# Graph network on one core: order of the own products, bf16 planes and register reads in the three mean layers

## The chip, the core and the metric

The program runs on one core of a Trainium2 chip. The metric is the device time of one execution in microseconds (us). The kernel before has a median of 7610.16 us over three runs (7602.88 to 7610.16).

## What is computed

Four graph modules follow each other over 6250 nodes with 128 features and 106250 edges (both directions of 50000 edges, and a loop at each node), sorted by destination. After each module there is a residual and a layer norm. The change concerns the third module alone, three "mean" layers:

```python
def sage_conv(h, Wl, b, Wr):
    agg = jax.ops.segment_sum(h[src], dst, num_segments=n) * inv_deg
    return agg @ Wl + b + h @ Wr
h = jax.nn.relu(sage_conv(x, W_l0, b0, W_r0))
h = jax.nn.relu(sage_conv(h, W_l1, b1, W_r1))
return sage_conv(h, W_l2, b2, W_r2)
```

The other modules (a gated recurrent layer, three attention layers, a tensor-product message layer) have the same text before and after.

## The kernel before, in words

Nodes lie in 49 blocks of 128, in 13 groups of four blocks (the last has one). Below, layers 0, 1 and 2 are the three mean layers. Each sums the rows of source nodes into a buffer of destination columns (`agg`, the first part of `sums`), in two ways.

- **Dense.** An adjacency matrix in bf16, made earlier, lies in DRAM. TensorE multiplies it with the node rows, which are split into three bf16 planes (line 1925), so that the float32 value is kept. There are 115 steps (`pe_dense`). The first 17 hold three blocks each and give 544 "extra" columns, one for each of 544 tiles of edges; the other 98 are two halves of 49 blocks with 5 banks of 418 columns. The queue of SyncE reads the adjacency through four slots.
- **Sums of a quad.** 288 tiles of 128 edges are gathered by GpSimd (line 1939, one indirect DMA each), four to a quad, 72 quads. ScalarE makes one-hot matrices (lines 1947, 1950), TensorE multiplies (line 1961, three banks in turn), and VectorE adds each of the four results to a window of `agg` whose start column is read from memory into a register (`window_at`, line 741, one load for four starts; the add is line 2026). Gathers use 16 slots: quad q+4 is gathered once quad q is multiplied. TensorE may be three quads ahead of VectorE's adds.
- **Extra adds.** The 544 extra columns are copied from the banks after step 17 (`keep_extras`, line 2009), and VectorE adds them one column at a time at register addresses (line 1992), 8 after each quad's adds, four starts to a register load. Each add to `agg` waits for the one before it, since windows can overlap. The halves of the dense part are added by `add_half` (line 2001), and line 2035 closes the layer.

Ahead of the sums comes a layer's head. In layers 1 and 2 TensorE makes the product of the last sums (line 1825), VectorE mixes it with the "own" term (line 1834), ScalarE applies Relu (line 2155) and issues the store of the rows. TensorE turns the rows (line 1856), ScalarE keeps them (line 1861) in `xT`; TensorE then makes the own product of a group (line 1871), and VectorE stores it with its bias (line 1880) in `hT`, over the node rows, for which reason a group's planes must be made first. Of a group's planes ScalarE makes the first, a bf16 copy (lines 2160, 2090), and VectorE the other two and a rest (lines 1845, 1846, 1848). TensorE puts up to 13 dense steps between the turns and own products. VectorE sets `agg` to zero (line 2147, in layer 0 line 2077). In layer 0 the head is the layer norm of the module before.

The order is that of the code. Each engine has its own queue and waits on semaphores. `quads_by(n)` says how many quads TensorE has multiplied after n dense steps: before the change none until step 13, and then 72 spread over 102 steps.

## Time and profile before

| what | us |
|---|---|
| median of the runs | 7610.16 |
| the profiled execution, whole | 7606.87 |
| its span | 7605.1 |
| layer 0 of the mean layers, 5054 to 5507.4 (with the norm) | 453.4 |
| layer 1, 5507.4 to 5940.7 | 433.3 |
| layer 2, 5940.7 to 6387.8 | 447.1 |

The page gives the busy time of each engine over the whole span. Which engine sets the pace of a stage is not read from it, but from the timelines: an engine can be idle half of the time between instructions that wait for each other. A timeline row merges equal instructions: its start, the time from the first start to the last end, their number, and in brackets the idle time ahead and what ended it. Register loads belong to the sequencer and don't count as busy.

### The profile page before, as it was taken

What the parts mean: (1) busy time and instruction counts of PE and PEld (TensorE: products, weight loads), DVE (VectorE), ACT (ScalarE), POOL (GpSimd) and SP (SyncE); (2) the same over time, 40 slices, a digit from 0 to 9 for tenths busy, and PEclk for the clock granted to TensorE, in tenths of its full rate; (3) what the DMA queues carried; (4) which work ended last, traced back from release to release, by engine and by line L of the source; (5) the groups of instructions that cost most, each with busy time, mean ns of one, the idle gap of its engine ahead of it and who ended that gap; (6) DMA issues with size and microseconds to landing.
All of it is one profiled execution on the core that took longest, in us unless ns stands there. A gap on an engine that the chain in (4) does not pass through costs nothing. (4 is left out here: it accounts for less than half of the span.)

```text
span 7605.1 us, 137273 instructions
## 1 busy us (share of the span) xinstructions
PE 5586.2 (73%) x30113; PEld 4217.7 (55%) x30114; DVE 4809.0 (63%) x20423; ACT 2121.2 (28%) x5508; POOL 5100.1 (67%) x5173
## 2 busy tenths in 40 slices
PE   5664454667767777776777766769899897898887
PEld 4432223345656655666655556656566654676665
DVE  7974433555666655666754766674454545888887
ACT  1033332131111141111141111143343332555554
POOL 5788772447777747777747777737657474777774
PEclk6687777877888787888887888889999998989988
DMA  9422232146677746777746767756667574222222
GB/s 308 122 68 63 71 76 53 36 126 197 205 207 205 205 148 194 208 206 205 209 152 188 210 206 206 206 151 207 176 198 211 161 216 120 55 55 55 55 54 52
DMA packets 911521, 1149.47 MB, mean 151 GB/s; under 512 B 143137, under 2 KB 676193, under 8 KB 911009
## 3 DMA queue, kind: packets, MB, share of 16 engines
q1 hardware_dynamic: 689200, 673.54, 29.4%
q0 software_dynamic: 202464, 461.07, 22.6%
q10 hardware_dynamic: 19346, 9.66, 0.5%
q14 instruction: 388, 3.18, 0.1%
q8 instruction: 123, 2.02, 0.1%
HBM read 882.09 MB, written 261.74 MB: 150 GB/s over the span
## 5 line engine op out<-in xcount | busy, mean ns | idle before, releaser
L486 POOL DMA_INDIRECT G<-table_kv,idx x2496 | 2377.4, 952 | 959.1 <-issue 762.3
L1554 DVE SCALAR_TENSOR_TENSOR sums<-ramp,place,bank 128x128 f32<-128x128 f32 x2496 | 721.9, 343 | 1001.1 <-PE bank L1501 813.5
L1939 POOL DMA_INDIRECT G<-table_h,src_idx x864 | 824.6, 954 | 485.4 <-issue 256.3
L1473 ACT COPY slab<-bank 128x512 f32<-128x512 f32 x624 | 364.9, 585 | 2485.0 <-PE bank L1492 2480.4
L1492 PE MATMUL bank<-ident,G 128*128 128x128 f32 x2496 | 627.7, 338 | 570.9 <-DMA G<-table_kv,idx 565.2
L1501 PE MATMUL bank<-qT,slab 128*128 x4992 | 916.2, 341 | 166.1 <-issue 144.4
L486 POOL DMA_INDIRECT G<-table_h,idx x832 | 835.4, 1004 | 299.3 <-issue 231.3
L534 PE MATMUL bank<-OH,sums 128*128 128x128 f32 x4992 | 858.7, 327 | 143.4 <-DVE sums L523 122.1
L1501 PEld LDWEIGHTS bank<-qT,slab 128*128 128x128 f32 x4992 | 810.6, 246 | 258.4 <-issue 257.9
L514 DVE TENSOR_SCALAR OH<-ramp,place,weight 128x128 f32<-128x128 f32 x2262 | 805.2, 359 | 151.2 <-issue 81.2
L534 PEld LDWEIGHTS bank<-OH,sums 128*128 128x128 f32 x4992 | 763.7, 234 | 195.0 <-issue 73.0
L1492 PEld LDWEIGHTS bank<-ident,G 128*128 128x128 f32 x2496 | 388.6, 167 | 762.5 <-DMA G<-table_kv,idx 725.0
L868 POOL DMA_INDIRECT adjacency<-sums x544 | 657.2, 1208 | 165.8 <-issue 165.8
L523 DVE TENSOR_TENSOR sums<-sums,bank 128x128 f32 x2496 | 697.4, 279 | 48.7 <-DVE sums L523 18.1
L1925 PE MATMUL bank<-sums,qT 128*128 128x418 bf16 (+1 forms) x3528 | 673.7, 333 | 31.6 <-DVEq L2004 10.9
L2401 PEld LDWEIGHTS bank<-OH,qT 128*128 128x128 f32 x3328 | 471.5, 225 | 283.0 <-DVE sums L2479 252.7
L2401 PE MATMUL bank<-OH,qT 128*128 128x128 f32 x3328 | 506.1, 315 | 123.9 <-DVE sums L2479 122.3
L849 POOL DMA_INDIRECT G<-table_gated,src_idx x288 | 284.1, 987 | 307.3 <-PE bank L973 176.2
L1925 PEld LDWEIGHTS bank<-sums,qT 128*128 128x128 bf16 x3528 | 346.7, 98 | 255.6 <-issue 35.7
L1992 DVE TENSOR_TENSOR sums<-sums,rows 128x1 f32 x1632 | 265.7, 163 | 347.8 <-DVE sums L2026 108.6
L1947 ACT ACTIVATE OH<-ramp,place 128x128 f32<-128x128 f32 x864 | 275.8, 390 | 676.1 <-PE bank L1961 674.1
L997 PE MATMUL bank<-slab,hT 128*128 128x418 f32 (+1 forms) x592 | 244.3, 566 | 294.9 <-DVE slab L1088 294.8
(342 smaller groups left out, 8868.2 us busy)
## 6 DMA issues: line engine op xcount, KB each, us to landing
stash<-G SPq DMA_DIRECT2D x312, 512.0 KB
sums<-stash SPq DMA_DIRECT2D x624, 256.0 KB
sums<-adjacency SPq DMA_DIRECT2D x294, 522.5 KB
adjacency<-same SPq DMA_DIRECT2D x49, 1184.0 KB
same<-adjacency SPq DMA_DIRECT2D x90, 522.5 KB
G<-table_kv,idx POOLq DMA_INDIRECT x2496
sums<-adjacency SPq DMA_DIRECT2D x48, 408.0 KB
table_kv<-G SPq DMA_DIRECT2D x72, 256.0 KB, 3.1
```

The lines of the kernel that those rows point to most:

```text
L486: pool.indirect_dma_start(G[:, s, 0:width], None, tab, bass.IndirectOffsetOnAxis(ap=idx[:, s:s + 1], axis=0)).then_inc(c_gather[s].sem, 16)
L514: ins = dve.tensor_scalar(OH[:, s, :], ramp[:], place[:, tile], w, ALU.is_equal, ALU.mult)
L523: dve.tensor_tensor(w, w, bank[banks[q_add % len(banks)]][:, k * P:(k + 1) * P], ALU.add).then_inc(c_added.sem, 1)
L534: ins = pe.matmul(bank[banks[q % len(banks)]][:, (s % QUAD) * P:(s % QUAD + 1) * P], view[:, s, :], OH[:, s, :], start=True, stop=True)
L868: pool.indirect_dma_start(adj_cells, bass.IndirectOffsetOnAxis(ap=cell[:, d:d + 1], axis=0), count[:, d:d + 1], None).then_inc(scattered[i ...
L1473: act.copy(quad(KT, q).rearrange("p s d -> p (s d)"), bank[q % 2][:, :]).then_inc(c_kt.sem, 1)
L1492: ins = pe.transpose(bank[q % 2][:, (s % QUAD) * P:(s % QUAD + 1) * P], G[:, s, 0:D], ident[:])
L1501: ins = pe.matmul(bank[2 + q % 2][:, (s % QUAD) * P:(s % QUAD + 1) * P], KT[:, s, :], w, start=True, stop=True)
L1554: ins = dve.scalar_tensor_tensor(scratch[:, s % QUAD, :], ramp[:], place[:, bass.ds(t * SLOTS + s, 1)], bank[2 + q % 2][:, (s % QUAD) * P: ...
L1925: ins = pe.matmul(bank[c][:, 0:width], plane[k][:, b * P:(b + 1) * P], adj_slot[s][:, j * at + c * width:j * at + (c + 1) * width], start= ...
L1939: pool.indirect_dma_start(G[:, s, 0:D], None, table[l], bass.IndirectOffsetOnAxis(ap=src_idx[:, DENSE + t:DENSE + t + 1], axis=0)).then_in ...
L2401: ins = pe.matmul(o, msg[:, s, part * D:(part + 1) * D], OH[:, s, :], start=True, stop=True)
```

## The change

The own term goes to `xT`, where the turned rows stood, so that it no longer overwrites the node rows. Own products come ahead of nearly all planes. VectorE makes the first plane, no longer ScalarE. GpSimd sets `agg` to zero behind its 16th gather. TensorE does no dense step before all own products are done; `pe_all_sums` then runs 115 steps with 2 quads ahead and 70 spread over all of them. The extra columns come 12, 8, 8 after a quad, from quad 12 on (before: 8, from quad 4 on). All register loads of a quad, two or three for its extra columns and one for its windows, are read ahead of the wait for TensorE. In layer 2 the residual is loaded into `nodes_h`.

```diff
+        own_h = xT[:].rearrange("p (b d) -> p b d", d=D)
...
-                                               nodes_h[:, b0 + j, :], ALU.mult, ALU.add)
+                                               own_h[:, b0 + j, :], ALU.mult, ALU.add)
...
-            dve.tensor_tensor(hT[:, four(g)].rearrange("p (b d) -> p b d", d=D),
+            dve.tensor_tensor(xT[:, four(g)].rearrange("p (b d) -> p b d", d=D),
...
+        def dve_first_planes(ready):
+            for g in range(GROUPS):
+                b0, nb = blocks_of(g)
+                ready(g, b0 + nb - 1)
+                dve.tensor_copy(plane[0][:, four(g)], hT[:, four(g)]).then_inc(first_plane.sem, 1)
 
         def dve_own_and_planes(l):
+            dve_planes(0)
+            done = 1
             for g in range(GROUPS):
                 dve_own(g, l)
-                if g + PLANES_AHEAD < GROUPS:
-                    dve_planes(g + PLANES_AHEAD)
+                if g % 3 == 2:
+                    dve_planes(done)
+                    done += 1
+            for g in range(done, GROUPS):
+                dve_planes(g)
...
-            return 2 + (n - GROUPS) * (RUN_QUADS - 2) // (STEPS - GROUPS) if n > GROUPS else 0
+            return 2 + n * (RUN_QUADS - 2) // STEPS
...
+                if t == SLOTS - 1:
+                    sums_used()
+                    pool.memset(agg, 0.0).then_inc(agg_zero.sem, 1)
...
+        def pe_all_sums():
+            for q in range(quads_by(0)):
+                pe_sum_quad(q)
+            for n in range(STEPS):
+                pe_dense(n)
+                for q in range(quads_by(n), quads_by(n + 1)):
+                    pe_sum_quad(q)
...
-        EXTRAS_A_QUAD = 8
+        def extras_by(q):
+            n = max(0, q - EARLY_QUADS)
+            return min(DENSE, 8 * n + 4 * -(-n // 3))
...
                 windows = window_at(DVE, DENSE + q * QUAD, QUAD)
+                columns = [c for d in range(extras_by(q), extras_by(q + 1), QUAD) for c in window_at(DVE, d, QUAD)]
+                if q == 0:
+                    dve.wait_ge(agg_zero.sem, agg_zero.at(1))
                 dve.wait_ge(c_rows.sem, c_rows.at(q + 1))
...
-                if q >= EARLY_QUADS and extras_left[0]:
-                    add_extras(min(EXTRAS_A_QUAD, extras_left[0]))
+                if columns:
+                    add_extras(extras_by(q), columns)
...
-                        sp.wait_ge(own_rows.sem, own_rows.at(GROUPS))
-                        sp.dma_start(xT[:].rearrange("p (b d) -> p b d", d=D), table[0].rearrange("(b p) d -> p b d", p=P)).then_inc(residual_in.sem, 16)
+                        sp.wait_ge(planes_ready.sem, planes_ready.at(GROUPS))
+                        sp.wait_ge(rows_stored.sem, rows_stored.at(16 * ROW_STORES))
+                        sp.dma_start(nodes_h, table[0].rearrange("(b p) d -> p b d", p=P)).then_inc(residual_in.sem, 16)
```

On TensorE, in layer 1 before, an own product of a group (line 1871) and a dense step (line 1925, three blocks) take turns:

```order
L1871 MATMUL bank<-wts,xT 128x128 [waits own_kept,turned_kept]
L1871 MATMUL bank<-wts,xT 128x128 x3
L1925 MATMUL bank<-sums,qT 128x272 [waits planes_ready,adjacency_in2]
L1925 MATMUL bank<-sums,qT 128x272 x3
L1925 MATMUL bank<-sums,same 128x272 x2
```

At the same place after the change the last own product (now line 1874) is followed by the sums of quads 0 and 1 (line 1976), and the first dense step (line 1937) stands behind these:

```order
L1874 MATMUL bank<-wts,xT 128x128 [waits own_kept,turned_kept]
L1976 MATMUL bank<-OH,G 128x128 [waits gather0,own_kept,onehot_ready]
L1976 MATMUL bank<-OH,G 128x128 [waits gather1]
L1976 MATMUL bank<-OH,G 128x128 [waits gather2]
L1976 MATMUL bank<-OH,G 128x128 [waits gather3]
L1976 MATMUL bank<-OH,G 128x128 [waits gather4,own_kept,onehot_ready]
L1976 MATMUL bank<-OH,G 128x128 [waits gather5]
L1976 MATMUL bank<-OH,G 128x128 [waits gather6]
L1976 MATMUL bank<-OH,G 128x128 [waits gather7]
L1937 MATMUL bank<-sums,qT 128x272 [waits planes_ready,adjacency_in0]
```

So 13 dense steps moved from among the turns and own products to behind them, and quads start at once.

On VectorE, before, each register load of a quad stands where its addresses are used (rows that repeat are left out; ISA is the register arithmetic of an address):

```order
L741 TENSOR_LOAD start
L2026 ISA [waits added,extra_added,rows_used]
L2026 TENSOR_TENSOR sums<-sums,bank 128x128
...
L741 TENSOR_LOAD start [waits added]
L1992 ISA [waits extra_added]
L1992 TENSOR_TENSOR sums<-sums,rows 128x1
```

After the change three or four loads stand in a row ahead of a quad's first wait:

```order
L742 TENSOR_LOAD start x4
L2051 ISA [waits added,extra_added,rows_used]
L2051 TENSOR_TENSOR sums<-sums,bank 128x128
...
L2014 ISA [waits extra_added,added]
L2014 TENSOR_TENSOR sums<-sums,rows 128x1
```

The number of loads is the same, 72 for windows and 136 for extra columns a layer; the latter moved from among the adds and extra adds to the front of the quad.

## Rows read from the trace of the kernel before

**Rows 1.** The page: busy time, share of the span and instructions of each engine.

```profile
PE 5586.2 (73%) x30113; PEld 4217.7 (55%) x30114; DVE 4809.0 (63%) x20423; ACT 2121.2 (28%) x5508; POOL 5100.1 (67%) x5173
```

**Rows 2.** Busy by stretch: stretch, length, PE, PEld, DVE, ACT, POOL, PEclk, DMA, GB/s.

```profile
5528.50:5532.60 4.10, 4.05 (x19) 2.81 (x20) 4.03 (x7) 0.87 (x2) 2.99 (x4) 0.50 0.19 51
5590.50:5745.50 155.00, 153.22 (x949) 98.46 (x948) 75.86 (x373) 61.16 (x161) 117.21 (x125) 1.00 0.72 213
```

**Rows 3.** VectorE timeline, a quad late in layer 1: start, length, group, [idle before].

```profile
5886.39 1.54 DVE L2026 TENSOR_TENSOR sums<-sums,bank 128x128 f32 x4 [0.45 <-DVE sums L1992]
5888.46 1.03 DVE L1992 TENSOR_TENSOR sums<-sums,rows 128x1 f32 x4 [0.52 <-DVE sums L2026]
5889.85 1.03 DVE L1992 TENSOR_TENSOR sums<-sums,rows 128x1 f32 x4 [0.35 <-DVE sums L1992]
5891.33 0.71 DVE L2026 TENSOR_TENSOR sums<-sums,bank 128x128 f32 x2 [0.45 <-DVE sums L1992]
```

**Rows 4.** Register loads on VectorE, 5600 to 5900: durations, first and last start.

```profile
L741 DVEq TENSOR_LOAD <-start x177: 339/343/375, 5599.9 to 5899.6; - x177
```

**Rows 5.** VectorE, layer 1: adds of quads 0, 1 and 4, the end.

```profile
5577.40 1.54 DVE L2026 TENSOR_TENSOR sums<-sums,bank 128x128 f32 x4 [2.43 <-PE bank L1961]
5579.25 1.55 DVE L2026 TENSOR_TENSOR sums<-sums,bank 128x128 f32 x4 [0.30 <-DVE sums L2026]
5590.53 1.12 DVE L2026 TENSOR_TENSOR sums<-sums,bank 128x128 f32 x3 [4.00 <-PE bank L1961]
5936.43 3.48 DVE L2001 TENSOR_TENSOR sums<-sums,bank 128x418 f32 x5 [0.41 <-DVE sums L1992]
5940.06 0.59 DVE L2035 TENSOR_TENSOR sums<-sums 128x418 f32<-128x418 f32 x1
```

**Rows 6.** TensorE: first sums of layers 0 and 1, dense steps of both kinds.

```profile
5142.87 1.83 PE L1961 MATMUL bank<-OH,G 128*128 128x128 f32 x15
5576.21 1.95 PE L1961 MATMUL bank<-OH,G 128*128 128x128 f32 x16
5577.99 0.63 PE L1925 MATMUL bank<-sums,qT 128*128 128x272 bf16 x4
5580.11 1.05 PE L1961 MATMUL bank<-OH,G 128*128 128x128 f32 x8
5895.62 1.95 PE L1925 MATMUL bank<-sums,qT 128*128 128x418 bf16 x10
5898.29 0.88 PE L1925 MATMUL bank<-sums,qT 128*128 128x418 bf16 x4
```

**Rows 7.** ScalarE: end of the norm, last Relu, a cast, a kept group.

```profile
5090.51 2.16 ACT L2090 CAST qT<-hT 128x512 bf16<-128x512 f32 x4
5525.01 0.31 ACT L2155 ACTIVATE hT<-hT 128x128 f32<-128x128 f32 x1 [0.44 <-ACT hT L2155]
5526.74 0.62 ACT L2160 CAST qT<-hT 128x512 bf16<-128x512 f32 x1
5527.26 0.59 ACT L1861 COPY xT<-bank 128x512 f32<-128x512 f32 x1
```

**Rows 8.** VectorE, head of layer 1: one plane operation of two groups.

```profile
5526.39 0.69 DVE L1845 TENSOR_TENSOR sums<-hT,qT 128x512 f32<-128x512 f32 x1 [2.77 <-ACT qT L2160]
5528.33 0.68 DVE L1845 TENSOR_TENSOR sums<-hT,qT 128x512 f32<-128x512 f32 x1
```

**Rows 9.** Groups by line: a single-source operation on VectorE, a memset on GpSimd.

```profile
L1218 DVE TENSOR_SCALAR start<-start 128x832 int32<-128x832 int32 x1 | 0.6, 587 | 0.0
L2265 POOL MEMSET wts<- 128x768 f32 x1 | 0.7, 737 | 41.8 <-PE bank L1825 41.8
```

**Rows 10.** GpSimd, gathers of layer 1: durations, first and last start.

```profile
L1939 POOL DMA_INDIRECT G<-table_h,src_idx x272: 939/944/953, 5577.5 to 5915.9; - x136
```

**Rows 11.** Layer 2: both engines at the adjacency read behind the residual.

```profile
6107.53 3.67 PE L1925 MATMUL bank<-sums,qT 128*128 128x418 bf16 x10 [4.46 <-DMA sums<-adjacency]
6116.88 1.13 DVE L2026 TENSOR_TENSOR sums<-sums,bank 128x128 f32 x3 [8.29 <-PE bank L1961]
```

More of the change, by code:

```diff
@@ L250, in build_program @@
         first_plane = signal("first_plane_ready")
+        agg_zero = signal("sums_zero")
         planes_ready = signal("planes_ready")
@@ L1979, in after_extra, with add_extras @@
                     dve.wait_ge(c_extra.sem, c_extra.at(n[1]))
-            extras_left = [DENSE]
-            def add_extras(k):
+            def add_extras(first, columns):
                 after_adds()
-                done = DENSE - extras_left[0]
-                extras_left[0] -= k
-                for d in range(done, done + k, QUAD):
-                    windows = window_at(DVE, d, QUAD)
-                    for j in range(QUAD):
-                        after_extra()
-                        w = agg[:, bass.ds(windows[j], 1)]
-                        dve.tensor_tensor(w, w, extra[:, d + j:d + j + 1], ALU.add).then_inc(c_extra.sem, 1)
-                        n[1] += 1
+                for d, column in enumerate(columns, first):
+                    after_extra()
+                    w = agg[:, bass.ds(column, 1)]
+                    dve.tensor_tensor(w, w, extra[:, d:d + 1], ALU.add).then_inc(c_extra.sem, 1)
+                    n[1] += 1
             def add_half(half):
@@ L2027, in dve_sums @@
                     n[0] += 1
-                if q >= EARLY_QUADS and extras_left[0]:
-                    add_extras(min(EXTRAS_A_QUAD, extras_left[0]))
+                if columns:
+                    add_extras(extras_by(q), columns)
                 if l == 2 and q == half_quads + 4:
                     dve.wait_ge(residual_in.sem, residual_in.at(16))
-                    dve.tensor_tensor(hT[:], hT[:], xT[:], ALU.add)
+                    dve.tensor_tensor(xT[:], xT[:], hT[:], ALU.add)
             add_half(1)
@@ L2076, in _, with normalized @@
                 dve.sem_inc(order_ready.sem, 1)
-                dve.memset(agg, 0.0)
-                for g in range(PLANES_AHEAD):
-                    dve_planes(g)
+                def normalized(g, b):
+                    dve.wait_ge(norm_dve.sem, norm_dve.at(b // 2 + 1))
+                    dve.wait_ge(norm_act.sem, norm_act.at((b + 1) // 2))
+                dve_first_planes(normalized)
                 dve_own_and_planes(0)
@@ L2086, in _ @@
                 for g in range(GROUPS):
-                    b0, nb = blocks_of(g)
-                    act.wait_ge(norm_dve.sem, norm_dve.at((b0 + nb - 1) // 2 + 1))
-                    act.wait_ge(norm_act.sem, norm_act.at((b0 + nb) // 2))
-                    act.copy(plane[0][:, four(g)], hT[:, four(g)]).then_inc(first_plane.sem, 1)
-                    if g >= 3:
-                        act_keep_turned(g - 3)
-                for g in range(GROUPS - 3, GROUPS):
                     act_keep_turned(g)
@@ L2106, in _ @@
                     pe_turn(g, normalized)
-                n = 0
                 for g in range(GROUPS):
                     pe_own(g, 0)
-                    if n < GROUPS:
-                        pe_dense(n)
-                        n += 1
-                for n in range(n, STEPS):
-                    pe_dense(n)
-                    for q in range(quads_by(n), quads_by(n + 1)):
-                        pe_sum_quad(q)
+                pe_all_sums()
         norm_passed()
@@ L2138, in _ @@
                 def _(_e):
-                    pool_rows(l)
+                    pool_rows(l, lambda: pool.wait_ge(filled.sem, filled.at(GROUPS)))
                 @block.vector
@@ L2144, in _ @@
                         dve_mix(g, PRODUCT_BANKS[g % 3])
-                    for g in range(PLANES_AHEAD):
-                        dve_planes(g)
-                    dve.memset(agg, 0.0)
+                    dve_first_planes(lambda g, b: dve.wait_ge(rows_ready.sem, rows_ready.at(g + 1)))
                     dve_own_and_planes(l)
@@ L2159, in _ @@
                     for g in range(GROUPS):
-                        act.copy(plane[0][:, four(g)], hT[:, four(g)]).then_inc(first_plane.sem, 1)
                         act_keep_turned(g)
@@ L2165, in _ @@
                 def _(_e):
-                    n = 0
                     for g in range(GROUPS):
@@ L2170, in _ @@
                         pe_turn(g, lambda g, b: pe.wait_ge(rows_ready.sem, rows_ready.at(g + 1)))
-                        while (n + 1) * FIRST_BLOCKS <= g // 2 * QUAD and n + 1 < GROUPS // 2:
-                            pe_dense(n)
-                            n += 1
                     for g in range(GROUPS):
                         pe_own(g, l)
-                        if n < GROUPS:
-                            pe_dense(n)
-                            n += 1
-                    for n in range(n, STEPS):
-                        pe_dense(n)
-                        for q in range(quads_by(n), quads_by(n + 1)):
-                            pe_sum_quad(q)
+                    pe_all_sums()
             sums_passed()
```

10 lines of the change are left out of this document (4 added, 6 removed).

## The prediction

> **What bounds the kernel now.** I read the page first, then the busy times by stretch, then the timelines of the mean layers, which is where the reader should look, too. By the page TensorE is the busiest engine, 73% [rows 1], and in the first part of layer 1's sums it is busy 153.2 of 155 us, VectorE only 75.9 [rows 2]. That reading misleads. In the timeline of VectorE each add waits for the one before it, and nothing else [rows 3]: four adds, a register load, four extra adds, a load, four extra adds, a load, and the next quad's adds begin 4.94 us after those before (5886.39 to 5891.33), with no wait for TensorE in brackets. Two other engines are close: TensorE needs 1.5 half steps of 2.67 us and one quad of 0.89, 4.9 us [rows 6]; a gather starts every 1.25 us (5577.5 to 5915.9, 271 steps), 5.0 us a quad [rows 10]. So three engines run in step, and VectorE, with the extra adds to do, holds the layer's end: from the first add of quad 4 at 5590.5 to the last operation's end at 5940.65 are 350.1 us [rows 5].
>
> The parts of VectorE's 4.94 us are needed below [rows 3]. Starts of adds are (1.54 - 0.29) / 3 = 0.42 apart (the last add alone is 0.29), of extra adds (1.03 - 0.16) / 3 = 0.29. From the first add to the first extra add are 2.07: a load after the adds costs 2.07 - 4 x 0.42 = 0.39. That is the load's own 0.343 [rows 4] and 0.05 around it. From one group of extra adds to the next are 1.39, so the load between them costs 1.39 - 4 x 0.29 = 0.23, since it partly lies beside an extra add that runs.
>
> **The change, part by part.**
>
> *Register reads.* What TensorE has ready costs VectorE no wait, so reading ahead of the wait hides nothing while VectorE is the late one [rows 3]. It even costs: the load that stood between extra adds for 0.23 now stands behind another load. No row shows two loads in a row. Below, it could be 0.05, the gap alone, if loads overlapped; above, 0.39, a load in series [rows 3, 4]. I take 0.39, the row nearest: after the adds the load also delays what stands behind it by its whole length. 133 such loads a layer (136 less the three of quad 12, which fall into a wait) at 0.39 are 51.9 us; before, 68 x 0.39 + 68 x 0.23 = 42.1. Plus 9.8. A quad with 8 extra columns now takes 5.1 us, one with 12 takes 6.3 (four more extra adds at 0.29), and the one ahead of it 5.5 for its fourth load: 16.9 for three.
>
> *The head.* In layer 1 the last Relu ends at 5525.3 [rows 7]. Before, ScalarE made a cast and a kept group in turn, 0.50 each; now 13 kept groups alone, 6.5 us, and an own product of 0.9 on TensorE: the first own result can be stored at about 5533. VectorE meanwhile makes 13 first planes from 5523.7 on. A copy of 512 float32 to bf16 is not in the trace. Below, it takes 512/832 of 0.587, 0.36 [rows 9]; above, 0.65, as a plane operation does. Even at 0.65 it is done, with one group of planes, by 5534: no cost in layer 1, and 0 to 3 us in layer 0, where the norm ends at 5090.5 [rows 7]; I take 1.5. From 5532.7 (5525.3 + 6.5 + 0.9) come 12.25 own results at 0.61 to 0.65 (8 us) and four groups of planes at 1.94 [rows 8] (7.8), and about 1.5 for the handovers: the last own result is stored at 5550.0, and quad 0 starts there, against 5576.2 before [rows 6]. That is 26.2 earlier. Layer 2 has the same head. Layer 0: 5090.5 + 6.5 + 0.9 + 1.5 + 17.3 = 5116.7, against 5142.9, also 26.2 earlier.
>
> *What is no longer done in the head.* Before, 13 dense steps ran among the own products, and the extra columns were ready 14.3 us after quad 0 (quad 4's first add at 5590.5, 5576.2 for quad 0). Now TensorE has all of it behind quad 0: 17 steps of 2.12 (5577.99 to 5580.11), 36.0; quads 0 to 12, 13 x 0.89 = 11.6; two half steps, 5.3 [rows 6]. Two waits come in. Quad 3 needs quad 0 added, and VectorE first has eight groups of planes to make (14.4, a load and adds 1.9), while TensorE is at quad 3 after 11.1: 5.2 us. And the extra columns are copied behind the adds of quad 11: 2.6. Together 60.7 from quad 0 to the first add of quad 12, 46.4 more than the 14.3 before.
>
> *What is left from there.* Eight quads are already added, at 1.85 each [rows 5]: 14.8 us less; the loads add 9.8. So 350.1 becomes 345.1, 5.0 less.
>
> *The zeroing.* GpSimd's memset of 768 elements took 0.74 [rows 9], which gives 6 us for 6668 in proportion. It stands behind the 16th gather (about 5548) and ends ahead of VectorE's first add (about 5566). Twice that would still end in time in layer 1, and cost 0 to 2 us in layer 0. VectorE's own memset lay in an idle stretch of the head; taking it off brings nothing but is contained in the head's sum. The Trainium skill ("GPSIMD Engine Reference", "Key points") says that GpSimd shares its SBUF interfaces with VectorE and contends with it where VectorE has two SBUF inputs, as the planes have; by it the upper figure is the likelier. No row here has the two side by side.
>
> *The residual.* In layer 2 the big read ahead of step 41 makes TensorE late, and VectorE waits 8.3 us [rows 11] (its cycle is 7.9 longer than 4.94). TensorE now needs 1.64 x 2.67 + 0.89 = 5.28 a quad where VectorE needs 5.64, and after 14 quads is 5.0 us ahead. That much of the wait goes.
>
> *Sum.* Layers 0 and 1: -26.2 + 46.4 - 5.0 = +15.2 each. Layer 2: 15.2 - 5.0 = +10.2. In all +40.6 on the profiled execution's 7606.9, 7647.5. The median of the runs shown is 3.3 above that execution, 7610.2, so the forecast is **7651**.
>
> **The rivals.**
>
> *A, the forecast:* VectorE stays the late engine, and starts its long stretch of extra adds 20 us later than before with only 5 us less to do.
>
> *B, loads cost little, TensorE sets the pace; faster.* If the sequencer takes the next load up while one is under way, a load in a row costs 0.05. VectorE's three quads then take 16.9 - 10 x 0.34 = 13.5 us, TensorE's 15.8, and TensorE has everything behind an earlier quad 0: 36.0 + 98 x 2.67 + 72 x 0.89 + waits of 10 are 371.8 us, then 6 for the last adds and the half (5936.43 to 5940.65 is most of it [rows 5]). Layer 1 ends at 5550.0 + 377.8 = 5927.8, 12.9 earlier, layer 0 12.8, layer 2 (which keeps its wait for the adjacency) 18.7 earlier, 44.4 in all: 7566. The total turns at 40.6 / 399 loads = 0.10 below my price, at 0.29 a load; below 0.28 TensorE is the bound. For it speaks that reading ahead of a wait is free where the wait is real, and that TensorE is busy 99% of a stretch already. Against it: behind a load the next instruction came a whole load later wherever the timeline lets me see it [rows 3], and the wait would have to be real, which it isn't.
>
> *C, the clock stays low in the head; slower still.* Before, dense steps kept TensorE busy through the head, and its granted clock was 1.00 afterwards, but 0.50 (the 1.2 GHz level) in the 4 us after its idle time [rows 2]. Now turns and own products alone fill three quarters of its time or less. At the lower level an own product of a group takes 1.8 us against the 1.2 that VectorE needs on average, 13 x 0.55 = 7 us later a layer, 21 in all: 7672. The Trainium skill ("TensorE: Matmul & The Clock Gate", "Part 1: The HAM clock gate") says that the clock follows how busy the engine has lately been; by it this case is possible, and the row of before agrees that idle time brings the lower level.
>
> *D, nothing measurable.* The head gains more than I see (a copy at 0.36, quad 3 not late because its planes end sooner), 10 to 13 us a layer: 7610 to 7620.
>
> **How the numbers follow.** Chances: A 0.60, B 0.15, C 0.15, D 0.10. Between A and C all is slower; B is faster; D is mostly within 0.2%, 15 us, which is about what a measurement of this kernel can tell from no change. Slower 0.75, same 0.08, faster 0.17. The unknown costs (0 to 9 for copies, 0 to 2 for the memset, -7 to +7 for my waits of a few us a layer) put A between 7627 and 7667. The range goes up past C to 7684 and down to 7590, which leaves out B.
>
> **What would show it.** Right: two or three quarters of the way through a layer VectorE shows a cycle of 5.1, 5.5 and 6.3 us a quad, no wait for TensorE in it, and TensorE idle between quads; loads in a row 0.39 apart; quad 0 in layer 1 about 43 us after the layer's start, where it was 69; quad 12's first add about 103 after it; layers of 469, 448 and 457 us. Wrong: VectorE's adds wait for TensorE's sums through the long stretch (B, and then the layer has 420 us), or loads in a row start 0.05 apart; TensorE at 0.50 while it turns rows and makes own products (C); quad 12 at less than 92 us (D). GpSimd should no longer be busy back to back.

## The result, and the profile after

The changed kernel takes 7642.87 us (median of 6 runs, 7633.51 to 7659.43), the kernel before in the same comparison 7606.68 (6 runs, 7594.99 to 7610.16). The ratio is 1.0052, with a 95% interval of 1.0039 to 1.0065: slower by half a per cent. Its profiled execution took 7643.14 us, with a span of 7641.3; the span before was 7605.1, so 36.2 us are to be explained.

I read the views in the same order as before. First the page's busy line, which answers to [rows 1]:

```profile
PE 5561.5 (73%) x30113; PEld 4192.3 (55%) x30114; DVE 4799.4 (63%) x20459; ACT 2105.1 (28%) x5469; POOL 5124.5 (67%) x5176
```

No engine's busy time has grown by more than 25 us: ScalarE has 16 less (its casts went), GpSimd 24 more (17.0 of it three memsets). The 36 us are waiting time and no work. The same holds of the stretch of [rows 2] in layer 1 (stretch, length, busy time of PE, PEld, DVE, ACT, POOL, then PEclk, DMA, GB/s):

```profile
5590.50:5745.50 155.00, 152.47 (x998) 102.43 (x996) 64.59 (x310) 57.22 (x150) 115.66 (x123) 0.99 0.74 217
```

TensorE looks as full as before, VectorE still emptier, and yet VectorE holds the end. Its timeline shows it. These are quads in that stretch (start, length, group, idle before), which answer to [rows 3]:

```profile
5702.17 1.55 DVE L2051 TENSOR_TENSOR sums<-sums,bank 128x128 f32 x4 [1.20 <-PE bank L1976]
...
5707.29 1.55 DVE L2051 TENSOR_TENSOR sums<-sums,bank 128x128 f32 x4 [1.20 <-issue]
5708.97 2.19 DVE L2014 TENSOR_TENSOR sums<-sums,rows 128x1 f32 x8
5712.73 1.54 DVE L2051 TENSOR_TENSOR sums<-sums,bank 128x128 f32 x4 [1.56 <-issue]
...
5715.63 2.49 DVE L2014 TENSOR_TENSOR sums<-sums,rows 128x1 f32 x9 [0.48 <-DVE sums L2014]
5719.31 1.55 DVE L2051 TENSOR_TENSOR sums<-sums,bank 128x128 f32 x4 [1.20 <-issue]
...
5724.38 1.55 DVE L2051 TENSOR_TENSOR sums<-sums,bank 128x128 f32 x4 [1.19 <-issue]
```

A quad with 8 extra columns takes 5.12 (5702.17 to 5707.29) and, at best, 5.07 us (5719.31 to 5724.38), the one with a fourth load behind it 5.44 (5707.29 to 5712.73). The one with 12 columns took 6.58 here, with a gap of 0.48 among its extra adds, and 6.24 where it has no such gap (5627.83 to 5634.07, in the next view of VectorE). The gap of 1.20 ahead of the adds is three register loads in a row, and 1.56 is four. "issue" means that no semaphore was late; where the brackets name TensorE the gap is no longer, so this wait is none either. The loads themselves, in the gap behind 5706.1 (durations, first and last start):

```profile
L742 DVEq TENSOR_LOAD <-start x3: 342/343/345, 5706.0 to 5706.7; - x3
```

Three loads start within 0.7 us. The fourth lengthens the gap from 1.20 to 1.56 and the quad from 5.07 to 5.44: a load in a row costs 0.37, its whole length and 0.03 more.

Now the head of layer 1, which starts where layer 0's last operation ends, at 5524.5, 17.2 later than in the kernel before. VectorE, answering to [rows 5] and [rows 8]: first planes, first own result, last plane, first add, the adds of quads 12 and 13, the end.

```profile
5539.85 4.24 DVE L1890 CAST qT<-hT 128x512 bf16<-128x512 f32 x13
...
5551.07 1.51 DVE L1882 TENSOR_TENSOR xT<-bank,bias_rows 128x512 f32<-128x512 f32 x2 [5.06 <-PE bank L1874]
...
5580.70 0.32 DVE L1851 TENSOR_TENSOR same<-sums,qT 128x128 bf16<-128x128 f32 x1
5581.28 1.54 DVE L2051 TENSOR_TENSOR sums<-sums,bank 128x128 f32 x4 [0.25 <-issue]
...
5627.83 1.55 DVE L2051 TENSOR_TENSOR sums<-sums,bank 128x128 f32 x4 [8.34 <-PE bank L1976]
...
5634.07 1.55 DVE L2051 TENSOR_TENSOR sums<-sums,bank 128x128 f32 x4 [1.20 <-issue]
...
5964.58 2.04 DVE L2023 TENSOR_TENSOR sums<-sums,bank 128x418 f32 x3 [0.50 <-DVE sums L2051]
5968.30 0.60 DVE L2060 TENSOR_TENSOR sums<-sums 128x418 f32<-128x418 f32 x1
```

And TensorE there, answering to [rows 6]: quads 0 and 1, the first dense step, quad 3, and the first half step behind the copy of the extra columns.

```profile
5566.86 3.75 PE L1976 MATMUL bank<-OH,G 128*128 128x128 f32 x16 [2.82 <-issue]
5570.41 1.11 PE L1937 MATMUL bank<-sums,qT 128*128 128x272 bf16 x4
...
5582.93 1.13 PE L1976 MATMUL bank<-OH,G 128*128 128x128 f32 x8 [2.27 <-issue]
...
5619.63 3.53 PE L1937 MATMUL bank<-sums,qT 128*128 128x418 bf16 x10 [2.53 <-DVE rows L2031]
```

Quad 0 stands 42.4 us behind the layer's start (5566.9 less 5524.5), where it was 68.9; quad 12's first add follows 61.0 behind quad 0; from there to the end are 341.1. So the layer took 444.4 us against 433.3. The three mean layers take 456.3, 444.4 and 454.1, where they took 448.0, 433.3 and 447.1: +8.3, +11.1 and +7.0, together 26.4 (layer 0 is counted here from its first operation on VectorE, shown below, and not from 5054 as in the table of before). Another 8.9 us lie ahead of them, in code that the change does not touch. The first operation of mean layer 0 on VectorE in the changed kernel, and then in the kernel before:

```profile
5068.23 2.23 DVE L2096 TENSOR_TENSOR qT<-hT,sums 128x448 f32<-128x448 f32 x4 [0.32 <-PEq L1711]
```

```profile
5059.29 2.23 DVE L2071 TENSOR_TENSOR qT<-hT,sums 128x448 f32<-128x448 f32 x4 [0.32 <-PEq L1710]
```

The remaining 1.0 us lies behind the mean layers (36.2 - 8.9 - 26.4).

### The profile page after: what moved, and what is told of

The parts are those of the page before. It is cut to its first block and busy times, and to the rows that moved or that the text cites. A ratio compares the mean times of both kernels' runs of the same rounds, so it can differ in the third digit from the quotient of the medians.

```text
span 7641.3 us, 137448 instructions
## 1 busy us (share of the span) xinstructions
PE 5561.5 (73%) x30113; PEld 4192.3 (55%) x30114; DVE 4799.4 (63%) x20459; ACT 2105.1 (28%) x5469; POOL 5124.5 (67%) x5176
## 5 line engine op out<-in xcount | busy, mean ns | idle before, releaser
L524 DVE TENSOR_TENSOR sums<-sums,bank 128x128 f32 x2496 | 697.8, 280 | 49.8 <-DVE sums L524 18.4
L2051 DVE TENSOR_TENSOR sums<-sums,bank 128x128 f32 x864 | 249.4, 289 | 403.5 <-issue 181.6
```

The lines of the kernel that those rows point to most:

```text
L524: dve.tensor_tensor(w, w, bank[banks[q_add % len(banks)]][:, k * P:(k + 1) * P], ALU.add).then_inc(c_added.sem, 1)
```

## The experiments

They ran on several chips. On one of them the kernel before took 7621.1 us, near its usual time; on others it took 10,127, 9,980 and 9,998. A kernel is only compared with the kernel before that ran beside it, and what the slow chips can and can't tell is said below. "Layer 1" is always from the end of the fold in layer 0 to the end of the fold in layer 1, as above.

### On the chip with the usual time

**Reads back in place.** The changed kernel with each read of four columns just ahead of its four adds:

```diff
-                for d, column in enumerate(columns, first):
-                    after_extra()
+                for g in range(first, last, QUAD):
+                    for d, column in enumerate(window_at(DVE, g, QUAD), g):
+                        after_extra()
```

> The kernel after with the reads of extra columns in their old place, each just ahead of its four adds (the first kernel again, beside the others of this call). Theory A: two or three reads a quad no longer stand in a row, each is 0.14 cheaper between extra adds, and the first no longer delays the next: VectorE's mean quad 5.4 instead of 5.59 us, some 8 to 11 us a layer, 24 to 30 in all: 7613 to 7619, ratio to before 1.001. Rival, reads ahead are free: unchanged, 7643, ratio 1.005.

Measured: 7621.99 us (10 runs), ratio to before 1.0002 (0.9992 to 1.0011). VectorE in this kernel, quads of 8 and of 12 extra columns:

```profile
5703.24 1.55 DVE L2051 TENSOR_TENSOR sums<-sums,bank 128x128 f32 x4 [0.45 <-DVE sums L2015]
5705.31 1.10 DVE L2015 TENSOR_TENSOR sums<-sums,rows 128x1 f32 x4 [0.53 <-DVE sums L2051]
5706.69 1.03 DVE L2015 TENSOR_TENSOR sums<-sums,rows 128x1 f32 x4 [0.28 <-DVE sums L2015]
5708.18 1.55 DVE L2051 TENSOR_TENSOR sums<-sums,bank 128x128 f32 x4 [0.45 <-DVE sums L2015]
...
5714.51 1.55 DVE L2051 TENSOR_TENSOR sums<-sums,bank 128x128 f32 x4 [0.45 <-DVE sums L2015]
```

4.94 us for 8 columns and 6.33 for 12: the mean of three quads is 5.40, where the changed kernel has (5.07 + 5.44 + 6.24) / 3 = 5.58. Times 58 quads that is 10.4 us. From quad 12 to the end layer 1 took 331.2 instead of 341.1, so 9.9 less, and the whole layer 436.4 instead of 444.4. The three layers together are 20.7 us shorter than in the changed kernel (7.1, 8.0 and 5.6), of the 26.4 that these had lost; 5.7 us remain. The changed kernel itself did not run in this comparison, but the one below with the zeroing on VectorE did, and its layer 1 took 341.4 us from quad 12 on, like the changed kernel's 341.1. With the reads back in place the kernel can't be told from the one before: the reading ahead is most of what makes the change slower, and the rest of it, which gains 26 us at quad 0, gives nothing in the end.

**No extra columns.** The changed kernel without the adds and reads of the extra columns:

```diff
-                columns = [c for d in range(extras_by(q), extras_by(q + 1), QUAD) for c in window_at(DVE, d, QUAD)]
...
-                if columns:
-                    add_extras(extras_by(q), columns)
```

> The kernel after, with the extra columns left out: none of the 544 single-column adds of a layer, and none of their 136 register reads. Their products are made on TensorE and copied, but not added, so the sums lack them. It asks who stands next behind VectorE. Theory A (VectorE is the late engine in the changed kernel, TensorE right behind it): VectorE's quad falls from 5.07, 5.45 and 6.24 us to some 2.5, and TensorE takes over with 36.0 + 98 x 2.67 + 72 x 0.89 + about 10 of waits and 6 of tail behind quad 0: a layer of 420 us instead of 444, so about 24 less in each of three, 7571 where the kernel after has 7643 (ratio to the kernel before 0.995). VectorE's adds then wait for TensorE's sums in every quad. Rival, TensorE is the late one already (the mean layers' 26 us come from TensorE's lost head start alone): the time stays within 5 us of the kernel after. Rival, gathers: the gather stream (1.25 us each, 288 of them, from 5564 on) sets the end, then a layer has 410 us and the kernel 7540.

Measured: 7590.23 us (4 runs), ratio 0.9958 (0.9942 to 0.9975); layer 1 took 425.2 us, and 320.8 of them from quad 12 on. VectorE in it, a quad between two half steps:

```profile
5704.75 1.55 DVE L2050 TENSOR_TENSOR sums<-sums,bank 128x128 f32 x4 [4.69 <-PE bank L1976]
5708.31 1.55 DVE L2050 TENSOR_TENSOR sums<-sums,bank 128x128 f32 x4 [2.01 <-PE bank L1976]
```

Here the waits for TensorE are real, 65 of them in the layer's 72 quads: the adds come 3.56 us apart, which is a half step of 2.67 and a quad of 0.89, or 6.23 where two half steps lie between. All of the extra columns' 87.5 us of busy time a layer went, and the layer is only 19.2 us shorter. So VectorE is the late engine of the changed kernel, and TensorE stands right behind it. Where the 19.2 us had lain is seen on TensorE. At the change of halves it waits for VectorE to read its banks, in layer 1 of the changed kernel (first line) and of this one (second):

```profile
PE bank L1937 <- DVEq L2026: 11.2, 1, 11.2
PE bank L1937 <- DVEq L2026: 3.4, 1, 3.4
```

That is 7.8 us less. Ahead of the next layer's first product TensorE stood idle for 16.7 us, now for 7.1, so 9.6 less; and two waits at quads, 1.8 us together, are gone: 19.2 in all. TensorE's account from quad 12's add to the end, without extra columns: 96 half steps of 2.67 and 59 quads of 0.89 are 308.8; 3.4 us it waits at the change of halves for its banks to be read, and 6 us are the tail. That is 318, against 320.8 measured. The gathers were no bound: a layer of 410 us would have been theirs.

**Reads beside adds, early waits away.** The changed kernel with three edits:

```diff
-            return 2 + n * (RUN_QUADS - 2) // STEPS
+            return min(2 + n * (RUN_QUADS - 2) // STEPS, max(3, n - 3))
...
-                if q == EARLY_QUADS:
+                if q == EARLY_QUADS - 1:
                     keep_extras()
...
-                columns = [c for d in range(extras_by(q), extras_by(q + 1), QUAD) for c in window_at(DVE, d, QUAD)]
+                groups, columns = list(range(extras_by(q), extras_by(q + 1), QUAD)), []
...
                     n[0] += 1
+                    if k < len(groups):
+                        columns += window_at(DVE, groups[k], QUAD)
```

> The kernel after with each read of four extra columns issued behind one of the quad's adds (as in the third kernel), and with the two waits of the head taken away: quad 3 is put behind the 7th dense step instead of the 4th, and quads 4 to 8 one behind each step, so that TensorE doesn't stand at quad 3 until VectorE has made its planes; and the extra columns are copied ahead of the adds of quad 11, not behind them. Theory A: the reads beside adds take VectorE's mean quad from 5.59 us to about 5.0, some 30 us of a layer, and the two waits were 5.2 and about 2 us; TensorE is next, at 412 us a layer against 444, so the kernel is at about 7547, ratio to before 0.992. Rival, the head's waits cost nothing because VectorE is late anyway: as the third kernel, 7565 to 7571. Rival, TensorE set the pace already: no gain from the reads, only up to 7 us a layer from the waits: 7622.

Measured: 7579.02 us (4 runs), ratio 0.9943 (0.9922 to 0.9963): faster than the kernel before and, by the ratios, than the changed kernel. VectorE, one quad of 12 columns and the start and end of one of 8:

```profile
5722.34 0.29 DVE L2051 TENSOR_TENSOR sums<-sums,bank 128x128 f32 x1 [1.04 <-PE bank L1976]
...
5724.28 3.44 DVE L2014 TENSOR_TENSOR sums<-sums,rows 128x1 f32 x12
5728.58 0.29 DVE L2051 TENSOR_TENSOR sums<-sums,bank 128x128 f32 x1 [0.85 <-PE bank L1976]
5729.08 0.29 DVE L2051 TENSOR_TENSOR sums<-sums,bank 128x128 f32 x1 [0.22 <-DVE sums L2051]
...
5730.43 2.21 DVE L2014 TENSOR_TENSOR sums<-sums,rows 128x1 f32 x8
5733.10 0.29 DVE L2051 TENSOR_TENSOR sums<-sums,bank 128x128 f32 x1 [0.46 <-DVE sums L2014]
```

With a load beside it an add starts 0.51 us behind the one before, not 0.42: the load costs 0.09 there instead of 0.37. The quad of 8 takes 4.52 us (5728.58 to 5733.10). TensorE in the same kernel has no gap in these rows:

```profile
5724.72 1.94 PE L1937 MATMUL bank<-sums,qT 128*128 128x418 bf16 x10
5726.50 1.05 PE L1937 MATMUL bank<-sums,same 128*128 128x418 bf16 x5
5727.39 1.05 PE L1976 MATMUL bank<-OH,G 128*128 128x128 f32 x8
```

From quad 12 on it took 320.9 us, the same as without any extra columns (320.8): all of their cost now lies beside TensorE. From quad 0 to quad 12's add were 55.1 instead of 61.0, so the two waits gave 5.9, against the 7 expected. I had expected this from waits of 5.2 and 2 us; in the changed kernel's trace they are 2.3 at quad 3 and 2.5 at the copy, and behind the second the half step at the lower clock (3.53 above, 1.94 in this kernel) took some 1.5 longer. The layer took 419.8 us and not the 412 expected, since I had left out three costs that remain: 3.4 us at the change of halves, 1.7 for gathers, and some 2.5 for a low clock at quad 0 (below).

**The zeroing back on VectorE.** The changed kernel with the memset between the first planes and the first group of planes on VectorE, and with neither the memset on GpSimd nor the wait for it:

```diff
                     dve_first_planes(lambda g, b: dve.wait_ge(rows_ready.sem, rows_ready.at(g + 1)))
+                    dve.memset(agg, 0.0)
                     dve_own_and_planes(l)
```

> The kernel after, with the sums zeroed by VectorE again, between the first planes and the first group of planes; nothing on GpSimd, and no wait for it. VectorE's memset of 6668 elements took 5.6 us in the kernel before, GpSimd's 5.7 in the kernel after. Theory (forecast: moving it gives nothing, it fits in idle time of the head): VectorE is through its first planes at about 19.6 us after the layer's start and has its first own result at 25.3; one group of planes, 1.94, and 5.6 of memset end at 27.1, so quad 0 comes 0 to 2 us later, and GpSimd's next gathers 0 to 5 earlier: in all 0 to +6 us against the kernel after. Rival, the memset is on the path, since VectorE has more to do in the head than it had before (13 first planes): +5.6 a layer, +17 in all. Rival, GpSimd's memset holds VectorE up through the shared interfaces: faster than the kernel after by 3 us a layer or more.

Measured: 7657.3 us (4 runs), ratio to before 1.0047 (1.003 to 1.0063), which can't be told from the changed kernel's 1.0052. Its head is more telling than its time. VectorE in layer 1, which starts at 5539.2 there:

```profile
5555.60 4.25 DVE L1890 CAST qT<-hT 128x512 bf16<-128x512 f32 x13
5561.19 5.62 DVE L2157 MEMSET sums<- 128x6668 f32 x1 [1.34 <-issue]
...
5568.59 1.88 DVE L1882 TENSOR_TENSOR xT<-bank,bias_rows 128x512 f32<-128x512 f32 x3
```

The first own result is stored 29.4 us behind the layer's start (5568.59 less 5539.2), where the changed kernel has it at 26.6: most of the memset lies in VectorE's idle 5.06 us, 2 to 3 us don't. Quad 0 came at 44.7 instead of 42.4, and the layers took 5.8, 2.6 and 1.0 us more than in the changed kernel's profile. So the memset on VectorE is not quite hidden in the new head: taking it off gives 2.3 us at quad 0, which my forecast had at nothing of its own. In the total this is less than the comparison can tell. Nothing spoke for the rival in which GpSimd's memset holds VectorE up.

### On the slow chips

Eight runs fell on chips on which every program of this case took about a third longer. There the kernels differed by less, and not in the same way.

**Reads in place, first time.** The same edit as above.

> The changed kernel with the register reads of the extra columns back where they are used (one behind the quad's adds, one between each four extra adds); the reads of the windows stay. Theory (VectorE sets the pace from quad 12 on, and a read in a row costs its whole length, 0.37 us in the changed kernel's trace): 67 reads a layer between extra adds fall from 0.37 to 0.23, 67 behind the adds go from 0.37 to 0.39: 8 us less a layer, some 24 in all, so about 12 us above the kernel before. A cycle of 8 extra columns 4.94, of 12 near 6.5 us. Rival (reads ahead of the wait are hidden, the time goes to TensorE's or GpSimd's new order): no gain over the changed kernel, or slower than it.

Measured: 10,097.9 us, ratio 0.9971 (0.9953 to 0.999), where the usual chip gave 1.0002.

**Before, with reads ahead.** The kernel before with this alone:

```diff
                 windows = window_at(DVE, DENSE + q * QUAD, QUAD)
+                first = max(0, q - EARLY_QUADS) * EXTRAS_A_QUAD
+                groups, columns = list(range(first, min(DENSE, first + EXTRAS_A_QUAD), QUAD)) if q >= EARLY_QUADS else [], []
+                for d in groups:
+                    columns += window_at(DVE, d, QUAD)
                 dve.wait_ge(c_rows.sem, c_rows.at(q + 1))
```

> The kernel before with this part of the change alone: both reads of a quad's extra columns stand behind the read of its windows, ahead of the wait for TensorE. Theory: 68 quads a layer of 5.07 us where 4.94 were, 8 to 9 us a layer more, some 25 in all (7632 where before has 7607). Rival (the reads hide in the wait): the same as before or faster.

> The kernel before with one part of the change alone: the reads of a quad's own and extra columns all stand ahead of its wait for TensorE; head, quads, zeroing and 8 extra columns a quad as before (the second kernel again, on a chip on which the kernel before has its usual time). Theory A: VectorE does not wait there, so three reads in a row cost 0.37 each where those between extra adds had cost 0.23: its quad takes 5.07 us, as the kernel after shows for 8 columns, instead of 4.94. Times 68 quads that is +9 us a layer, +26 in all, ratio 1.0035. Rival, reads ahead of a wait are free or better: ratio 1.000 or less. Rival, VectorE had slack before (the gathers at 5.0 us a quad set the pace, not its 4.94): +0.07 x 68, 5 us a layer, ratio 1.002.

Measured: 0.9997 (0.9977 to 1.0017) and 0.9989 (0.9973 to 1.0006), no difference. But its length of a quad on VectorE can be read wherever a quad does not wait, as here, in the second of the two:

```profile
7806.19 1.54 DVE L2024 TENSOR_TENSOR sums<-sums,bank 128x128 f32 x4 [2.77 <-remote]
7807.86 2.20 DVE L1986 TENSOR_TENSOR sums<-sums,rows 128x1 f32 x8
7811.26 1.54 DVE L2024 TENSOR_TENSOR sums<-sums,bank 128x128 f32 x4 [1.20 <-issue]
```

5.07 us, against 4.94 with the reads in place [rows 3]. The price of the edit is there; on this chip it is mostly covered, since in five of the eight quads around these rows the gap ahead of the adds is 2.1 to 2.9 us and ends with a sum.

**Beside the adds.** The changed kernel and the kernel before, each with the reads behind the quad's first adds (the last of the edits shown for the fastest kernel), and nothing else.

> The changed kernel with each read of four extra columns issued right behind one of the quad's adds of 128 columns, while that add runs. The read of quad 1's windows stood so in the kernel before and cost 0.16 us there. Theory: a cycle of 8 columns costs VectorE 4.65, of 12 columns 6.0, three quads 15.3 us against TensorE's 15.8: TensorE becomes the bound, and a layer ends about 13 us sooner than in the kernel before, 44 in all: 7563 where before has 7607. Rival (the head's new order, GpSimd's memset or the clock is what made the change slow): little gain over the changed kernel, 7620 to 7640.

> The same kernel as in e3 (the changed kernel with each read of four extra columns behind one of the quad's adds), since the first four ran on a chip where the kernel before took 10127 us, with idle time inside TensorE's dense steps that no semaphore ended. Where before takes about 7607, theory: TensorE sets the pace (15.8 us for three quads against VectorE's 15.3), 7563. Rival (not the register reads, but the head, the memset or the clock): 7620 to 7640. If before takes 10127 again, all kernels come within 0.5% of each other and the run settles nothing.

> The kernel after with the reads of extra columns behind the quad's first adds and nothing else (the third kernel again): it takes apart the two edits of the kernel with reads beside adds and without early waits, which had 0.9943 of the kernel before. Theory A: quad 12 stays at 103 us after the layer's start (the waits at quad 3 and at the copy of the extra columns are still there), and from there TensorE sets the pace with 321 us as in that kernel and in the one without extra columns: 424 us a layer, 20 less than the kernel after, ratio 0.9975. Rival, the early waits cost nothing: ratio 0.9943 as there. Rival, only the early waits had brought the gain: 1.0045.

> The kernel before with the same edit: both reads of extra columns stand behind the first two adds of a quad. Theory: VectorE's cycle falls from 4.94 to 4.65, below the 5.0 that four gathers take on GpSimd and the 4.9 of TensorE, so VectorE no longer lags three quads behind and a layer gains its lag, about 11 us, 33 in all (7574). If GpSimd or TensorE had set the pace all along, as the page's busy shares suggest, it gains nothing (7607).

> The kernel before with the reads of extra columns issued behind the quad's first two adds, so that they run beside them; nothing else changed (the fourth kernel again). In the third kernel's profile such a quad of 8 columns took about 4.6 us on VectorE. Theory A with the gathers next: GpSimd's gathers were back to back in the kernel before (16 in 20.0 us without a gap, 5.0 us a quad), and can't go faster, so a layer loses only what lies behind the last gather: about 421 us instead of 433, ratio 0.995; GpSimd busy back to back, VectorE waiting for TensorE's sums. Rival, TensorE next (4.90 a quad): 98 x 2.67 + 68 x 0.89 + 6 = 328 from quad 4 on instead of 350, 411 a layer, ratio 0.991. Rival, VectorE was not the late engine of the kernel before: ratio 1.000. Beside the best kernel so far (0.9943) this says whether the new order of the head is worth anything once the reads are hidden.

Measured: the changed kernel with it has 0.998 (0.9962 to 0.9997), 0.9963 (0.994 to 0.9986) and 0.9961 (0.9947 to 0.9976) in three comparisons; the kernel before with it 0.9993 (0.9969 to 1.0017) and 0.9996 (0.9978 to 1.0013). The first is faster than before in all three, the second in neither. The last two runs had asked what each of the fastest kernel's edits is worth, and whether the kernel before would be as fast with the reads alone; neither is answered for the usual chip. What can be said is local: the quad takes 4.50 us on VectorE in the kernel before, too (in the last of these runs):

```profile
7805.29 0.29 DVE L2022 TENSOR_TENSOR sums<-sums,bank 128x128 f32 x1 [3.30 <-remote]
...
7809.79 0.29 DVE L2022 TENSOR_TENSOR sums<-sums,bank 128x128 f32 x1 [0.42 <-issue]
```

What is different on these chips shows on TensorE. In the first profile with reads ahead in the kernel before, it stood idle in the middle of a half step (first fence), and the view of waits of layer 1 counts 80 such gaps (second: engine, line, what for, us in total, times, longest), where the kernel before has none on that line on its own chip:

```profile
7808.69 0.59 PE L1925 MATMUL bank<-sums,qT 128*128 128x418 bf16 x2
7811.08 0.34 PE L1925 MATMUL bank<-sums,qT 128*128 128x418 bf16 x1 [1.79 <-issue]
```

```profile
PE bank L1925 <- issue: 56.4, 80, 3.4
```

No semaphore ended these gaps, and they are no low clock: over 300 us of sums (7600 to 7900 in the last run of the kernel before beside adds) the granted clock was 0.97. VectorE's, ScalarE's and GpSimd's own durations were the same as on the usual chip (0.29 for an add, 0.95 for a gather). What holds TensorE's instructions back there stays open.

## Why the prediction was right, point by point

The forecast was 7651 and the time is 7642.87; the mechanism is the one foreseen, but two deviations of opposite sign stand in the sum, and I name them.

*Who bounds.* Right for the changed kernel. Without the extra columns the layer falls by 19 us, and VectorE then waits for TensorE in nearly every quad; with them its gaps behind quad 12 are the length of its loads, but for a few that are 0.3 to 0.7 longer. One sign that I gave is wrong: TensorE is not idle between quads. It waits there twice in layer 1, 1.8 us in all, and spends its lead at the change of halves (11.2 us) and behind its last quad (16.7). For the kernel before, the same reading of [rows 3] was not tested on a chip with the usual time; its trace shows the same sign, 21.3 us of idle time ahead of layer 2's first product, where the kernel without extra columns has 7.1.

*Reads ahead.* Right in kind and close in size. I took 0.39 for a load in series and it is 0.37, so the quads take 5.07, 5.44 and 6.24 us instead of 5.1, 5.5 and 6.3. Rival B, with 0.05, is out. My 9.8 a layer becomes 7.1 with a load at 0.37 (133 x 0.37 less 42.1). That is against the kernel before, which has 68 quads with extra columns. Put back in place in the changed kernel, with its 58 such quads, the reads cost 57 x 0.39 + 76 x 0.23 = 39.7, so the account gives 9.5; measured from quad 12 on are 9.6 in layer 0 and 9.9 in layer 1, and 5.4 in layer 2, which has the wait for the adjacency. The whole layers gave 7.1, 8.0 and 5.6, and in layers 0 and 1 most of the difference is TensorE's clock ahead of quad 12. In layer 1 of that profile it was 0.54 between quads 3 and 4, which took 4.7 us where the changed kernel's took 3.0; in layer 0 it was 0.53 in the half step behind the copy, 3.25 us for 1.79.

*The head.* Quad 0 came 26.5 us earlier in layer 1 (forecast 26.2), 27.9 in layer 0. The own results began at 26.6 behind the layer's start (25.4 forecast), and the 13 first planes took 4.24 us, 0.33 each on average, just under my lower bound of 0.36.

*What comes in its place.* From quad 0 to the first add of quad 12 I had 60.7; it is 61.0 in layer 1, and 59.5 and 59.7 in layers 0 and 2. The sum is right and one of its terms is not. TensorE waited 2.3 us at quad 3 and not 5.2, because it got there later: it stood idle for 2.82 us ahead of quad 0 and then ran quads 0 and 1 at half speed. Busy by stretch (columns as above), quads 0 and 1, then dense steps, and the first half step behind the copy of the extra columns:

```profile
5566.86:5570.41 3.55, 3.55 (x17) 3.49 (x17) 3.48 (x6) 1.43 (x5) 3.55 (x1) 0.50 0.02 5
5572.58:5580.66 8.08, 8.08 (x70) 6.64 (x67) 7.94 (x14) 2.05 (x6) 5.99 (x7) 1.00 0.65 159
5619.63:5622.95 3.32, 3.32 (x10) 1.45 (x11) 0.00 (x0) 0.00 (x0) 2.61 (x3) 0.52 0.48 164
```

3.55 us at a granted clock of 0.50 (1.2 GHz) for 16 matmuls that take 1.78 at 1.00, and the two steps behind them took 2.17 where two take 1.40. A little of rival C thus took place, 2.5 us in layer 1, and cost nothing there, since TensorE would have waited for VectorE's planes anyway. In layers 0 and 2 the same 16 matmuls took 2.87 us behind a gap of the same length, and the wait at quad 3 was 3.1. The half step behind the copy is another matter: in layer 1 it ran at 0.52 and took 3.32 us where the next takes 1.79, and VectorE waited for it. In layers 0 and 2 it ran at 1.00, which is the 1.3 to 1.5 us by which layer 1 is longer here. Over the head the clock's mean was 0.90, and it was 1.00 from 5550 to 5563, while the own products ran, so rival C as forecast is out. The Trainium skill ("TensorE: Matmul & The Clock Gate", "Part 1: The HAM clock gate") says the clock follows how busy the engine has been; this row agrees.

*What is left from quad 12.* 341.1 in layers 0 and 1, where I had 345.1: 9.0 less than before, not 5.0. Of the 4 us, 3 are the loads (20 threes of quads, each 0.15 shorter than 5.1 + 5.5 + 6.3).

*The zeroing.* 5.68 us on GpSimd for the 6 in proportion, done at 5571.1, ahead of the first add at 5581.3:

```profile
5565.44 5.68 POOL L1955 MEMSET sums<- 128x6668 f32 x1
```

VectorE made planes all that time, at 0.68 and 0.69 an operation, as in [rows 8]. The Trainium skill's contention ("GPSIMD Engine Reference", "Key points") does not show here: VectorE's operations were no longer than without it, and GpSimd's memset took no more than the 6 in proportion (the same memset never ran on GpSimd alone).

*The residual.* Wrong in size. I expected TensorE's lead to take 5.0 of the 8.3 us of [rows 11]; VectorE still stands for 7.7 there, 1.2 of which are its loads:

```profile
6150.45 3.67 PE L1937 MATMUL bank<-sums,qT 128*128 128x418 bf16 x10 [9.25 <-DMA sums<-adjacency]
6156.86 1.55 DVE L2051 TENSOR_TENSOR sums<-sums,bank 128x128 f32 x4 [7.68 <-PE bank L1976]
```

Without the loads in either gap (0.45 before, 1.20 now) the wait fell from 7.8 to 6.5 us, by 1.3; over all that follows quad 12 layer 2 gained 2.8 more than layer 1 (11.9 against 9.0). The lead was there: TensorE waited 9.25 us for the adjacency, 4.8 more than before. But it could not be used, since the step behind the wait started 22.0 us after the residual's read was issued (6128.41 to 6150.45), as it did before (21.7, 6085.82 to 6107.53): the DMA ends this wait, and TensorE's lead became its own idle time. What failed is that I took a lead of TensorE off VectorE's wait one for one.

*The sum.* Forecast for the three layers 15.2, 15.2 and 10.2, 40.6 in all; measured 8.3, 11.1 and 7.0, 26.4. I was 14.2 us too high where the change is: 9.8 for what follows quad 12 (4.0, 4.0 and 1.8), 2.4 for quad 0 and 2.0 for what lies between. The 8.9 us in front of the mean layers brought the total near the forecast again, and my prediction had nothing there: that part of the agreement is luck. The four kernels of the comparison where before took 7621.1 speak for scatter and not for the change. By their layers alone, against the 1328.4 us that the three take in the profile of before, they should be at 1.0007 (reads in place), 0.9956 (no extra columns), 1.0047 (zeroing on VectorE) and 0.9940 (reads beside adds); measured are 1.0002, 0.9958, 1.0047 and 0.9943. With 8.9 us more in front each would be 0.0012 higher, and reads in place at 1.0019 would lie outside its interval. This is an estimate, since the kernel before has no profile in that comparison. Without the 8.9 us the ratio would be nearer 1.004, still slower and in my range.

## What to carry to other kernels

Before hiding a register read ahead of a wait, look whether the wait exists: a gap whose releaser is "issue" or the engine's own last operation is not a wait, and a read put there is paid in full (0.37 us here); behind one of several dependent adds, which leave the engine free between them, it costs 0.09. An engine that is busy 99% of a stretch needn't be the bound: taking out the other engine's suspected work shows both who bounds and how far the next one is behind (here 20 us a layer; the best version got that and the 6 us of two waits in front). And when work is taken out of an idle stretch of one engine to start another stage earlier, count what that work will then displace: 26.5 us won at quad 0 cost 46.6 us in front of the extra columns.

## What the runs showed of the hardware that was not expected

- A register load behind another costs 0.37 us, at a length of 0.343. Beside a VectorE add in a chain of dependent adds, a load adds 0.09.
- The kernel before took 7607 and 7621 us in two comparisons, and 9,980 to 10,127 in three others, on other chips. TensorE's mean granted clock over the span was 0.84 on the former and 0.74 on the latter, with gaps within groups of matmuls that no semaphore ended; VectorE's durations were the same. Ratios changed with it: reads in place had 1.0002 on one and 0.9971 on the other. A comparison of half a per cent holds for the kind of chip it was made on. The changed kernel itself was never run on the slow ones, and whether the chip or its state at the time makes them slow is not shown.
- After 2.82 us of idle time TensorE's next 16 matmuls ran at the lower clock level in layer 1 (3.55 us) and only in part in layers 0 and 2 (2.87 us); after 2.53 us the next half step ran at 0.52 in layer 1 and at 1.00 in layer 0.
- The same read of adjacency behind the residual let TensorE go on 21.7 and 22.0 us after the residual's issue, whether TensorE had waited 4.46 or 9.25 us for it.
- A memset of 5.68 us on GpSimd beside two-input VectorE operations did not lengthen these (0.68 to 0.69 us with it and without).
